# Four slots in place of two for the down-projection weights of a transformer layer, on eight cores

## The reference

```python
# attention: 16 heads of 128, rope on q and k, softmax, output projection
x = layernorm(x + attn(x, wq, wk, wv, wo))
# feed-forward; the weights are integers 0..255, W = (wq - 128) * scale, HID = 5632
gate = silu(x @ Wgate.T)
up   = x @ Wup.T
x = layernorm(x + (gate * up) @ Wdown.T)
```

## Time and profile before

| | us |
|---|---|
| median of 3 runs | 4619.93 (4618.51 to 4622.57) |
| the profiled execution | 4624.43 |
| its span on the slowest core, core 5 | 4622.5 |
| spans of the other cores | 4605.6 to 4617.5 |
| down projection, eight column blocks on core 5, matmuls alone | 771.2 |

### The profile page before, as it was taken

One profiled execution on the slowest core, in us unless ns is written; L12 is line 12 of the kernel. 1 busy time (PEld: TensorE's weight loads), 2 busy tenths in 40 slices (PEclk: granted clock), 3 DMA queues, 4 the chain that ended last, 5 costly groups with the idle time before them and its releaser, 6 DMA issues.

```text
span 4622.5 us, 41881 instructions; the slowest of 8 cores (4605.6 to 4622.5 us)
## 1 busy us (share of the span) xinstructions
PE 3874.3 (84%) x15680; PEld 1487.0 (32%) x15680; DVE 608.3 (13%) x1312; ACT 1309.4 (28%) x1061; POOL 357.6 (8%) x680
## 2 busy tenths in 40 slices
PE   4999997777777777777977999988874999998872
PEld 1444442111111111112433444433321444443331
DVE  0222100000010000100220000011112000011112
ACT  0111113344433344333442333310005333320004
POOL 1000000000000000000000000012210000002220
PEclk8999998778887788878988999999997999999996
DMA  7334321110010010001575444454455444434453
GB/s 130 62 69 93 83 72 38 23 19 14 14 28 14 14 28 14 14 17 33 168 193 96 73 79 77 74 79 63 62 122 126 78 77 79 73 53 63 62 107 109
DMA packets 200710, 310.94 MB, mean 67 GB/s; under 512 B 99265, under 2 KB 152642, under 8 KB 191682
## 3 DMA queue, kind: packets, MB, share of 16 engines
q0 software_dynamic: 97344, 188.85, 25.6%
q1 hardware_dynamic: 98562, 115.22, 8.3%
q10 hardware_dynamic: 4608, 4.20, 0.3%
HBM read 412.86 MB, written 58.72 MB: 102 GB/s over the span
## 4 chain that ended last, share of the span: by engine, by line
PE 68%; DMA 16%; issue 6%; ACT 5%; DVE 5%; DVEq 0%; POOL 0%; ACTq 0%; SPq 0%; POOLq 0%
PE PS L600 13%; PE PS L593 13%; DMA AB<-wd_c 10%; PE PS L484 9%; PE PS L536 6%; PE PS L532 6%; PE PS L569 5%; PE PS L499 5%; PE PS L521 4%; ACT AB L659 3%; PE PS L614 3%; PE PS L524 3%; DMA AB<-AB 3%; DMA AB<-xT 2%; DVE AB L824 1%
## 5 line engine op out<-in xcount | busy, mean ns | idle before, releaser
L659 ACT ACTIVATE AB<-PS,AB 128x1024 bf16<-128x1024 f32 x512 | 563.9, 1113 | 853.4 <-PE PS L524 853.3
L614 PE MATMUL PS<-AB 128*128 128x512 bf16 x2816 | 669.3, 392 | 137.3 <-DVE AB L824 135.1
L593 PE MATMUL PS<-AB 128*128 128x512 bf16 x2816 | 634.6, 383 | 118.2 <-ACT AB L725 54.5
L600 PE MATMUL PS<-AB 128*128 128x512 bf16 x2816 | 623.1, 379 | 0.0
L484 PE MATMUL PS<-AB 128*128 128x512 bf16 x2048 | 450.7, 384 | 63.4 <-DMA AB<-xT 63.4
L521 PE MATMUL PS<-AB 128*128 128x512 bf16 x512 | 247.5, 483 | 291.2 <-DVE AB L771 277.1
L614 PEld LDWEIGHTS PS<-AB 128*128 128x128 bf16 x2816 | 269.0, 100 | 537.6 <-issue 275.0
L593 PEld LDWEIGHTS PS<-AB 128*128 128x128 bf16 x2816 | 275.4, 98 | 463.0 <-issue 137.3
L532 PE MATMUL PS<-AB 128*128 128x512 bf16 x896 | 394.0, 440 | 36.1 <-ACT AB L659 36.0
L600 PEld LDWEIGHTS PS<-AB 128*128 128x128 bf16 x2816 | 275.7, 98 | 333.5 <-issue 1.9
L536 PE MATMUL PS<-AB 128*1 128x512 bf16 x896 | 377.7, 422 | 0.0
(11 more groups left out here) (76 smaller groups left out, 1685.8 us busy)
## 6 DMA issues: line engine op xcount, KB each, us to landing
AB<-wg_c POOLq DMA_DIRECT2D x88, 512.0 KB, 6.3
AB<-wu_c POOLq DMA_DIRECT2D x88, 512.0 KB, 8.6
AB<-wd_c POOLq DMA_DIRECT2D x352, 128.0 KB, 2.9
AB<-x SPq DMA_DIRECT2D x16, 1024.0 KB, 6.7
x1f<-AB SPq DMA_DIRECT2D x16, 1024.0 KB, 4.0
AB<-x1f SPq DMA_DIRECT2D x16, 1024.0 KB, 6.4
out<-AB SPq DMA_DIRECT2D x16, 1024.0 KB, 6.3
AB<-xT POOLq DMA_DIRECT2D x16, 512.0 KB, 13.3
```

Source lines behind the costliest of these rows:

```text
L593: mm = t.matmul(bank(par * 4 + cch)[:, 0:512], GDQ[par][:, di * 128:(di + 1) * 128], X1T[:, di * 1024 + cch * 512: di * 1024 + (cch + 1) * ...
L600: mm = t.matmul(bank(par * 4 + 2 + cch)[:, 0:512], UDQ[par][:, di * 128:(di + 1) * 128], X1T[:, di * 1024 + cch * 512: di * 1024 + (cch + ...
L614: mm = t.matmul(bank(tt)[:, 0:512], HT[:, h2 * 1024 + tt * 128: h2 * 1024 + (tt + 1) * 128], WDQ[i % 2][:, 0:512], start=(h2 == 0), stop=( ...
L659: sc.activation(PT[u % 4], bank(2 * (u % 2), 2)[:, 0:1024], AF.Exp, bias=CVC[:, 0:1], scale=ASCL).then_inc(s2sc, 1)
```

## The change

Both sets of slots grow from two to four: `WDB` (what lands) and `WDQ` (what PE reads). Two offsets move to make room. POOL now waits for the dequant of block i - 4 instead of i - 2, and DVE for PE's block i - 4 instead of i - 2. The two landing semaphores `s4wd` stay two, and POOL still waits, from block 2 on, for the landing of transfer i - 2. The order of instructions on every engine is the same as before, with one wait more or less here and there; the lines behind the new one move down by one.

```diff
-OFF_WDQ   = 190464
-OFF_STAT4 = 192512
+OFF_WDQ   = 192512
+OFF_STAT4 = 196608
...
-    WDB = [bf16(OFF_WDB + i * 1024, 128, 512) for i in range(2)]
-    WDQ = [bf16(OFF_WDQ + i * 1024, 128, 512) for i in range(2)]
+    WDB = [bf16(OFF_WDB + i * 1024, 128, 512) for i in range(4)]
+    WDQ = [bf16(OFF_WDQ + i * 1024, 128, 512) for i in range(4)]
...
                         i = (th * 4 + dc) * NHT + h2
+                        if i >= 4:
+                            g.wait_ge(s4wq, i - 3)
                         if i >= 2:
-                            g.wait_ge(s4wq, i - 1)
                             g.wait_ge(s4wd[i % 2], 16 * (i // 2))
-                        g.dma_start(out=WDB[i % 2], in_=wd_h[h2, dc]).then_inc(s4wd[i % 2], 16)
+                        g.dma_start(out=WDB[i % 4], in_=wd_h[h2, dc]).then_inc(s4wd[i % 2], 16)
...
-                                          WDQ[i % 2][:, 0:512],
+                                          WDQ[i % 4][:, 0:512],
...
                         v.wait_ge(s4wd[i % 2], 16 * (i // 2 + 1))
-                        if i >= 2:
-                            v.wait_ge(s4dn, i - 1)
-                        v.tensor_scalar(WDQ[i % 2], WDB[i % 2], -128.0, None,
+                        if i >= 4:
+                            v.wait_ge(s4dn, i - 3)
+                        v.tensor_scalar(WDQ[i % 4], WDB[i % 4], -128.0, None,
                                         AL.add).then_inc(s4wq, 1)
```

## The result

The changed kernel takes 4534.0 us (median of 9 runs) against 4622.5 for the kernel before (10 runs, the first three with it); the ratio is 0.981, 95% interval 0.9798 to 0.9822, so 82 to 93 us less. 4535 was predicted. Some executions show a lower granted clock on one die or both and take longer, and all ratios here compare only the others.

A forecast was written before the change was run, and what follows sets the result against it. The ring of load, dequant and issue (3.91 us per two blocks, PE needs 3.45) was taken as the bound. Savings 50 + 13 + 22 = 85 took 4624.4 to 4539.4, or 4535 for the median; range 4505 to 4572.

The forecast's parts named there:

- The ring sets the pace: Down projection: load, dequant, signals and issue take 3.91 us per two blocks, PE needs 3.45; the change shortens it 0.46 to 0.52.
- Quiet column blocks: Column blocks 2, 3, 5, 6, 7 of the down projection: PE becomes the bound; 50 us saved.
- the slow start after a seam: Quiet blocks except 5: first 16 matmuls after the emptying run at the lower granted clock, 2.7 to 3.0 us more.
- Column block 1: First column block, beside 16 transposing transfers: the shorter ring saves 13 us, bounds 5 and 24.7.
- Blocks 4 and 8: Column blocks with eight residual loads beside the weight loads: 11 us saved in each, 22 for both.
- The sum, 85: Saving over the eight column blocks of the down projection: 50 + 13 + 22 = 85 us.
- PE's idle time: Idle time ahead of the down matmuls falls from 137.3 to some 60 us, including six emptying gaps of 5.3.
- The other signs: Profile signs: quiet windows 76 to 80 us, dequant waiting for PE there, blocks 4 and 8 at 100 to 104.
- Rival (b): Shortened ring gets longer elsewhere, by issues beside dequants or longer loads; 40 us gained, 4580; chance 0.12.
- Rival (c): Nearly everything goes: PE at its pace in all eight column blocks, 628 us, 143 less, 4477; chance 0.06.
- Rival (d): The change does nothing, since the landing wait is what holds POOL; time stays 4620; chance 0.04.
- Rival (e): Slower: weight loads bunch in pairs and lock at 4.89 us each, ring 5.43, 4805; chance 0.04.

The follow-up runs named there:

- wdb4_only: Changed kernel with the dequantized slots (WDQ) back at two, so only the landing slots (WDB) grow to four; ratio 0.9811, 4535 us.
- wdq4_only: Only WDQ grows to four; WDB and POOL's wait stay as in the kernel before; no ratio, its one comparable execution, the profiled one, took 4641.0 us.
- after_extra_dequant: Changed kernel with a useless second dequant of 384 of 512 columns ahead of each real one; ratio 0.9823, 4541 us.
- four_in_flight: Changed kernel with four landing semaphores, one for each slot, so four weight loads can be in flight instead of two; ratio 0.9693, 4481 us.
- early_dequant_again: Repeat of: four_in_flight with the next column block's first three dequants before the emptying, PE waiting for each bank alone; ratio 0.9648, 4460 us.

## Why the prediction was right

- *The ring sets the pace* (the dequant, POOL's wait behind it and the load, 3.91 for two blocks against PE's 3.45). Shown by wdb4_only, wdq4_only and the two kernels with an extra dequant.
- *Quiet column blocks, 50 forecast.* 444.2 to 389.2, 55 measured. PE is the bound, as said. The size is short by 5: 1 was rounded off the sum of 51, and the slow start after a seam cost 1.4 to 2.8 us in blocks 2, 3, 6 and 7 and not 2.7 to 3.0. In this profile 6 to 12 matmuls ran 0.43 us apart there, the pace of the lower clock.
- *Column block 1, 13 forecast.* 100.7 to 91.2, 9.5 measured. *Blocks 4 and 8, 22 forecast.* 226.3 to 199.1, 27.2 measured. These sizes depend on the core: of all eight cores before, core 5 had the longest blocks 4 and 8. On the average of all cores the three terms are 54.5, 10.4 and 24.6. Residual loads come closer together, as said: the timeline of SP has 66.23 us for the eight in place of the 78.14 of the earlier trace rows,

```profile
3345.68 66.23 SPq L374 DMA_DIRECT2D AB<-x1f  x8
```

that is 9.5 us for four weight blocks where I had 11.1 - 1.0. The direction of that term was sound, its size was an argument and not a measurement.
- *The sum, 85.* 91.7 in the column blocks of the two profiles, 87.2 in their spans, 88.5 in the medians. Errors of +5, -3.5 and +5 stand behind a total that looks better than its parts. That 4534.0 met 4535 to 1 us is luck besides: I subtracted from a median of 4620 of three runs, and over ten it is 4622.5.
- *PE's idle time* was forecast at 60 and is 77.6: six seams of 5.3 make 32, and I left 28 for the rest, where blocks 1, 4 and 8 have 42 and the two starts of the stage 3.5. The other signs came as named or close to it: quiet blocks at 76 to 79 and loads there of 2.9 us (median over all cores), blocks 4 and 8 at 100.3 and 98.8 for the 100 to 104 named.
- *Rival (b)*, a longer ring elsewhere, is out by after_extra_dequant and by the load times of the quiet blocks. *Rival (c)*, nearly all of it, came with four_in_flight: 622.2 for the eight against the 628 worked out for it, and what it needed was what I held against it, more than two loads in flight. *Rival (d)*, that the change does nothing because the landing wait binds, is out as a whole; but that wait did bind in 1, 4 and 8 once the dequant was off the ring. *Rival (e)*, bunching: the pair issued together after each start does not lock. On core 0 of the changed kernel 12 pairs are issued within 0.7 us in block 4 (two are the x2 rows above), as against 14 on core 5 before, and 3 to 7 in each quiet block, whose loads stay at 2.9.

## What to carry to other kernels

Count every wait that a load's issue stands behind, and put the slot's ring (load, landing, use, issue) beside what the consumer needs for the same slots; the gain of more slots ends at the first wait that did not grow with them. Here slots went from two to four and landing semaphores stayed two, and that wait alone held back another 54 us. More slots behind the converting engine gave some 3 us at most while the ring ahead of it was the bound.

## What the runs showed of the hardware

Weight loads that overlap a 1 MB residual load took 4.5 us on average in column blocks 4 and 8 of the changed kernel (all cores, up to 7.7), those of quiet blocks 3.0. With four in flight they took 5.2, longer still, and yet PE was supplied, at 176 GB/s: late loads cost nothing here once enough others were under way. A PE that gets one matmul each 0.6 us through a seam kept the upper clock at 12 of 48 seams of early_dequant_again and lost it at 36. And the profile names the last of two releasers to end, which for POOL was a dequant of 0.29 us inside the 0.54 that it needs from a landing to an issue; a start 0.08 after the named releaser, where a true release takes 0.60, gives it away.
